# A mixture-of-experts stage cut into 63 tiles of 256 rows and nine of 128, in place of 71 tiles of 256

## The chip, the cores and the metric

The kernel runs on one core of one Trainium2 chip. The metric is the device time of one execution in microseconds. The core has five engines with their own instruction streams: TensorE (PE, matmuls; PEld are its weight loads), VectorE (DVE), ScalarE (ACT), GpSimd (POOL) and SyncE (SP), and 16 DMA engines that all of them feed.

## What is computed

The reference is one layer of a language model over 64 sequences of 128 tokens, with 192 channels:

```python
h = tok(x, adj_cooc, ...)            # embeddings + three graph vectors, projection, layer norm
h = h + attn(layernorm(h))           # a long convolution along each sequence
h = h + ffn(layernorm(h))            # mixture of experts, below

# ffn: E = 8 experts, F = 768 hidden, top 2
router_logits = einsum('th,eh->te', xf, Wr)
topk_vals, topk_idx = top_k(router_logits, 2)
routing_weights = softmax(topk_vals)
h = gelu(einsum('th,efh->etf', xf, Wi) + bi)      # each expert: 192 -> 768 -> 192
expert_out = einsum('etf,ehf->eth', h, Wo) + bo
out = sum over the 2 chosen experts of weight * expert_out
```

8,192 tokens choose two experts each, so 16,384 rows go through the experts. The change is in this last part alone.

## The kernel before

Up to about 460 us the kernel makes h, stores it to `out` in DRAM (`store_rows`), and stores each token's normalised row with its two routing weights in a table `xtab_d`. The experts' weights lie split in a high and a low bf16 part in `blob_d`, 1.44 MB each.

**Placement.** VectorE turns the experts' row counts (bank 0) and each row's rank within its expert (bank 7) into a slot for every row (`sl`, line 1280). An expert's rows begin at a tile's start, so it takes its count, rounded up to 256. `NT` = 71 tiles hold the worst case, and `NC` = 142 blocks of 128 slots. `eid[q]` is the expert of tile q; a tile that no expert needs takes expert 7. A one-hot matmul loop of 16 turns (VectorE line 1297, ScalarE line 956, TensorE line 741) then inverts the slots into a table of row ids, `id_g` to gather with and `id_s` to scatter with. Unused slots scatter to spare rows behind the output.

**Expert stage.** Tile q passes through the engines so, each in its own program order:

- GpSimd: `fetch(q)` gathers two blocks of 128 rows from `xtab_d` (two DMAs, line 537); `add_rows(q)` adds two blocks of results to `out` in DRAM (two accumulating scatters, line 551). In the turn of tile q it issues `fetch(q + 5)` and then `add_rows(q - 2)`. A token's two results are added by different tiles, so a tile's scatters wait until those of the two tiles before it have landed in DRAM. For the last `LATE` = 8 tiles the wait for the tile just before falls away if it has the same expert (`held`).
- ScalarE: `row_hi(q + 1)` (line 963) splits a gathered tile, then `hidden(q)`: twelve gelu activations (lines 975, 976) that end each half bank of the up projection.
- VectorE: `row_lo(q + 1)` (lines 1346, 1347), `split_hidden(q)` (line 1362, three times), `transposed(q + 1)` (line 1351) and `bias_out(q - 1)` (lines 1372, 1376). `bias_out(q)` writes into one of `RY` = 4 output buffers, so it waits until the scatters of tile q - 4 have landed.
- TensorE: `up_tile(q)`, 30 matmuls of 256 columns (lines 780 to 784), `turn_rows(q + 1)`, six transposes (line 763), `down_tile(q - 1)`, 36 matmuls of 192 columns (lines 799 to 801), half of them for each block of 128 rows.
- SyncE: two weight buffers, used by even and by odd tiles. Before tile q it compares `eid[q]` with `eid[q - 2]`, and only if they differ it loads the up part (line 458, 771 KB, once the gelus of tile q - 2 are done) and the down part (line 461, 672 KB, once `bias_out(q - 2)` has read its bias):

```python
sp.wait_ge(gelu, FC // 2 * (q - WB + 1))
with sp.If(e != held):
    load_up(e, w)
```

The inputs are drawn with a fixed seed. Running the reference on them gives the experts 554, 3420, 325, 0, 2312, 718, 2992 and 6063 rows. Before, they take 3, 14, 2, 0, 10, 3, 12 and 24 tiles, 68 in all, and three tiles are empty. `eid[q]` differs from `eid[q - 2]` at twelve tiles: 3, 4, 17 to 20, 29, 30, 32, 33, 44 and 45.

Of the kernel before, what the change touches and what calls it, by code (L numbers as in the profile page):

```python
# [6 lines left out]
B, S, D = 64, 128, 192  # L7
V = 30522
GRAPHS, GD = 3, 16
E, F = 8, 768  # L10
# [11 lines left out]
TS = 256  # L22
NT = (2 * B * S + E * (TS - 1)) // TS
NC = NT * TS // 128
# [12 lines left out]
W3 = 3  # L37
WB = 2
# [3 lines left out]
RX = 6  # L42
# [13 lines left out]
LATE = 8  # L56


def tower(nc, t, out):
# [3 lines left out]
    with ctx:  # L63
# [55 lines left out]
        cst = sb("cst", [128, 128 + 128 + 256 + 128 + 1 + NC + 2 * TG])  # L119
# [13 lines left out]
        onesf = sb("onesf", [128, E])  # L133
# [74 lines left out]
        cnt = carve(4 * E).rearrange("p (a e) -> p a e", a=4)  # L208
# [5 lines left out]
        cnti = sb("cnti", [128, 2, E], i32)  # L214
# [10 lines left out]
        late = sb("late", [1, LATE], i32)  # L225
# [116 lines left out]
        def landed_by(q):  # L342

            return 16 * (q // 2 + 1)
# [6 lines left out]
        def _(sp):  # L351
# [148 lines left out]
            for h in range(2):  # L500
                for a in range(2):
                    sp.wait_ge(scat[h][a], landed_by(NT - 1 - (NT - 1 - a) % 2))

        @block.gpsimd
        def _(pool):
# [28 lines left out]
            def fetch(q):  # L534
                after(pool, hid, q - RX + 1)
                for h in range(2):
                    pool.indirect_dma_start(xg_f[:, q % RX, h, :], None, xtab_d,  # L537
                                            bass.IndirectOffsetOnAxis(ap=id_g[:, 2 * q + h:2 * q + h + 1], axis=0)).then_inc(xg_in[q % RX], 16)

            def add_rows(q):  # L540

                before = held[q] if q in held else landed_by(q - 1)
                for h in range(2):
                    if q > 1:
                        pool.wait_ge(scat[h][q % 2], landed_by(q - 2))
                    if q > 0:
                        pool.wait_ge(scat[h][(q - 1) % 2], before)
                        pool.sem_inc(pool_turn, 1)
                pool.wait_ge(yo_ready, q + 1)
                for h in range(2):  # L550
                    pool.indirect_dma_start(out, bass.IndirectOffsetOnAxis(ap=id_s[:, 2 * q + h:2 * q + h + 1], axis=0), yo[:, q % RY, h, :], None,  # L551
                                            compute_op=ALU.add).then_inc(scat[h][q % 2], 16)
# [7 lines left out]
            held = {NT - LATE + k: pool.value_load(late[0:1, k:k + 1], min_val=landed_by(NT - LATE - 3), max_val=landed_by(NT - 2)) for k in range(LATE)}  # L560
# [12 lines left out]
        def _(pe):  # L573
# [184 lines left out]
            def turn_rows(q):  # L758

                pe.wait_ge(x_lo, q + 1)  # L760
                for h in range(2):
                    for c in range(3):
                        last = nc.tensor.transpose(xT_ps[:, c * TS + h * 128:c * TS + h * 128 + 128],  # L763
                                                   xs[:, q % 2, h, c * 128:(c + 1) * 128], identb[:, :])
                last.then_inc(xg_t, 1)

            def up_tile(q):
# [5 lines left out]
                x0, x1, x2 = (xgT[:, q % W3, c, :] for c in range(3))  # L773
                for f in range(FC):
                    if f % 2 == 0:
                        after(pe, gelu, FC // 2 * (q - 1) + f // 2 + 1)
                    ps = bank[2 + f // 2][:, (f % 2) * TS:(f % 2 + 1) * TS]
# [10 lines left out]
            def down_tile(q):  # L788
# [5 lines left out]
                for h in range(2):  # L794
# [19 lines left out]
        def _(act):  # L814
# [143 lines left out]

            def row_hi(q):

                act.wait_ge(xg_in[q % RX], 32 * (q // RX + 1))
                after(act, xg_t, q - 1)
                f(xs[:, q % 2, :, 0:D], xg_f[:, q % RX, :, 0:D], ACT.Copy).then_inc(x_hi, 1)
# [4 lines left out]
            def hidden(q, w):  # L968

                bi = parts(wbuf[q % WB])[2]  # L970
                for c in range(0, FC, 2):
                    act.wait_ge(up, FC // 2 * q + c // 2 + 1)
                    for d in (c, c + 1):
                        ps = bank[2 + c // 2][:, (d % 2) * TS:(d % 2 + 1) * TS]
                        f(hh[w][:, d, :], ps, ACT.Gelu, bias=bi[:, d:d + 1])  # L975
                        last = f(hf[w][:, d, :], ps, ACT.Gelu, bias=bi[:, d:d + 1])  # L976
                    last.then_inc(gelu, 1)
# [8 lines left out]
        def _(dve):  # L986
# [18 lines left out]
            v.memset(onesf[:, :], 1.0)  # L1005
# [262 lines left out]
            v.tensor_scalar(cnti[:, 0, :], bank[0][:, 0:E], float(TS - 1), None, ALU.add)  # L1268
            fence()
            v.tensor_scalar(cnti[:, 1, :], cnti[:, 0, :], 8, None, ALU.logical_shift_right)  # L1270
            fence()
            v.tensor_copy(cnt[:, 1, :], cnti[:, 1, :])
            fence()
            v.tensor_tensor_scan(cnt[:, 2, :], onesf[:, 0:E], cnt[:, 1, :], 0.0, ALU.mult, ALU.add)
# [24 lines left out]
            for g in range(TG):  # L1299
# [4 lines left out]
                if g == 1:  # L1304
                    dve.wait_ge(eid_turned, 1)
                    v.tensor_scalar(eid[:, :], bank[1][0:1, 0:NT], float(E - 1), None, ALU.min).then_inc(eid_done, 1)

            raw = bank[1][0:1, :]
            assert (NT - LATE) % 2 == 1
# [4 lines left out]
            v.scalar_tensor_tensor(marks[:, 2, :], marks[:, 0, :], E - 0.5, marks[:, 1, :], ALU.is_lt, ALU.mult)  # L1314
            fence()
            v.tensor_tensor(marks[:, 1, :].rearrange("o (k i) -> o k i", i=2), marks[:, 2, :].rearrange("o (k i) -> o k i", i=2),
                            repeat(cst[0:1, 256:256 + LATE // 2], 2, 2), ALU.add)
            fence()
            v.tensor_scalar(late[:, :], marks[:, 1, :], 16.0, float(landed_by(NT - LATE - 3)), ALU.mult, ALU.add)
# [23 lines left out]
            def row_lo(q):  # L1343
                dve.wait_ge(x_hi, q + 1)
                rows, split = xg_f[:, q % RX, :, :], xs[:, q % 2, :, :]
# [3 lines left out]
            def transposed(q, w):  # L1349
                dve.wait_ge(xg_t, q + 1)  # L1350
                v.tensor_copy(xgT[:, w, :, :], bank[0][:, :].bitcast(bf16)[:, 0:3 * TS].rearrange("p (c n) -> p c n", c=3)).then_inc(xgT_ready, 1)  # L1351

            def weights(q, w):

                for h in range(2):
                    v.scalar_tensor_tensor(wk[:, w, h:h + 1], xg_f[:, q % RX, h, D + 1:D + 2], row_k[:, 2 * q + h:2 * q + h + 1],
                                           xg_f[:, q % RX, h, D:D + 1], ALU.mult, ALU.add)

            def split_hidden(q, w, blocks):
                for c in blocks:  # L1360
                    dve.wait_ge(gelu, FC // 2 * q + c // 2 + 1)
                    last = v.tensor_tensor(hl[w][:, c:c + 2, :], hf[w][:, c:c + 2, :], hh[w][:, c:c + 2, :], ALU.subtract)  # L1362
                return last

            def bias_out(q):

                w, x = q % W3, q % RY
                for h in range(2):
                    if q >= RY:
                        dve.wait_ge(scat[h][q % 2], landed_by(q - RY))  # L1370
                dve.wait_ge(down, q + 1)
                v.tensor_tensor(yo[:, x, :, :], bank[5 + w][:, 0:2 * D].rearrange("p (h d) -> p h d", h=2),
                                repeat(parts(wbuf[q % WB])[5], 1, 2), ALU.add).then_inc(biased, 1)
                fence()
                for h in range(2):
# [72 lines left out]
```

## Time and profile before

| | us |
|---|---|
| runs without the profiler, median of 3 (lowest, highest) | 991.08 (987.75, 995.53) |
| span of the profiled execution, first to last instruction | 995.9 |
| first matmul of expert tile 0 | 502.44 |
| last matmul of the expert stage starts | 979.43 |
| last scatter issued | 987.85 |
| TensorE, VectorE, ScalarE, GpSimd busy | 869.3, 656.0, 536.0, 644.7 |

The page gives no separate device time of the profiled execution; its span is 4.8 us above the median of the other runs. A difference worked out within the span is applied to the median.

### The profile page before, as it was taken

To read this page: it belongs to the slowest core of one execution; us is meant where nothing else is said; L and a number is where in the kernel's file an instruction comes from. 1 tells how busy PE (TensorE), PEld (TensorE's weight loads), DVE (VectorE), ACT (ScalarE), POOL (GpSimd) and SP (SyncE) were. 2 spreads that over 40 slices of the span, in tenths; PEclk is the share of its full clock that TensorE was granted. 3 is DMA by queue.
4 is the path that set the end of the run, shared out by engine and by line. 5 is a ranking of instruction groups with operands and counts; after the bars stand their busy time and mean duration, and the time that the engine had idled before them with its cause. 6 is when DMAs were issued, how large, how long until landed. Compare 5 with 4: busy or idle time off the path is not lost.

```text
span 995.9 us, 22850 instructions
## 1 busy us (share of the span) xinstructions
PE 869.3 (87%) x7469; PEld 822.9 (83%) x7469; DVE 656.0 (66%) x2142; ACT 536.0 (54%) x1271; POOL 644.7 (65%) x552
## 2 busy tenths in 40 slices
PE   3959898998898739893889999999999999999993
PEld 2959898998898738892679999999999989898993
DVE  3167857776867565978756776666667656666662
ACT  1222223213312325599667777777777767677761
POOL 6777777777777300100067886777778768788886
PEclk9957556556756669996699999999999999999997
DMA  8437547457465429855946446745744543343454
GB/s 245 131 87 248 179 153 257 136 200 225 157 207 195 126 86 282 225 166 131 245 101 149 61 60 158 191 61 122 199 83 63 130 96 61 59 60 59 61 57 44
DMA packets 99788, 138.31 MB, mean 139 GB/s; under 512 B 13427, under 2 KB 81430, under 8 KB 97654
## 3 DMA queue, kind: packets, MB, share of 16 engines
q0 software_dynamic: 39552, 53.26, 28.1%
q1 hardware_dynamic: 59142, 73.59, 24.3%
q10 hardware_dynamic: 1008, 10.34, 2.8%
q8 instruction: 50, 0.82, 0.4%
q14 instruction: 36, 0.29, 0.1%
HBM read 98.14 MB, written 39.02 MB: 138 GB/s over the span
## 4 chain that ended last, share of the span: by engine, by line
PE 29%; DMA 22%; POOL 22%; issue 12%; DVE 8%; ACT 4%; DVEq 2%; SPq 1%; POOLq 0%; ACTq 0%
DMA out<-Hs,id_s 20%; POOL ev_g L521 13%; POOL emb_g L512 5%; PE bank L799 3%; PE bank L801 3%; PE bank L800 3%; POOL blob L537 3%; PE bank L780 2%; PE bank L781 2%; PE bank L784 2%; PE bank L783 2%; PE bank L782 2%; DVE hstats L1157 2%; ACT adj_s L956 1%; PE bank L763 1%
## 5 line engine op out<-in xcount | busy, mean ns | idle before, releaser
L975 ACT ACTIVATE Hs<-bank,U 128x256 bf16<-128x256 f32 x426 | 214.0, 502 | 126.0 <-PE bank L784 126.0
L551 POOL DMA_INDIRECT out<-Hs,id_s x142 | 233.5, 1645 | 65.6 <-issue 45.6
L537 POOL DMA_INDIRECT blob<-xtab_d,id_g x142 | 151.6, 1068 | 122.7 <-DVEq L1340 79.6
L521 POOL DMA_INDIRECT ev_g<-in_word_emb,ids_i x192 | 189.7, 988 | 58.5 <-issue 57.9
L976 ACT ACTIVATE Hs<-bank,U 128x256 f32<-128x256 f32 x426 | 216.4, 508 | 0.0
L799 PE MATMUL bank<-U,Hs 128*128 128x192 bf16 x852 | 210.0, 246 | 0.3 <-issue 0.3
L801 PE MATMUL bank<-U,Hs 128*128 128x192 bf16 x852 | 208.8, 245 | 0.0
L800 PE MATMUL bank<-U,Hs 128*128 128x192 bf16 x852 | 208.5, 245 | 0.0
L1362 DVE TENSOR_TENSOR Hs<-Hs 128x512 bf16<-128x512 f32 x213 | 146.8, 691 | 92.1 <-ACT Hs L976 92.0
L780 PE MATMUL bank<-wst,U 128*128 128x256 bf16 x426 | 116.6, 274 | 1.3 <-DVE wst L1351 1.3
L781 PE MATMUL bank<-wst,U 128*128 128x256 bf16 x426 | 116.7, 274 | 0.0
L782 PE MATMUL bank<-wst,U 128*128 128x256 bf16 x426 | 116.6, 274 | 0.0
L784 PE MATMUL bank<-wst,U 128*128 128x256 bf16 x426 | 116.6, 274 | 0.0
L783 PE MATMUL bank<-wst,U 128*128 128x256 bf16 x426 | 116.6, 274 | 0.0
L621 PE MATMUL bank<-cs,ev_g 128*128 128x1 f32 x384 | 91.2, 307 | 3.2 <-DMA ev_g<-in_word_emb,ids_i 3.1
L622 PE MATMUL bank<-cs,ev_g 128*128 128x1 f32 x384 | 92.6, 311 | 0.0
L621 PEld LDWEIGHTS bank<-cs,ev_g 128*128 128x128 f32 x384 | 84.0, 270 | 3.4 <-DMA ev_g<-in_word_emb,ids_i 3.4
L622 PEld LDWEIGHTS bank<-cs,ev_g 128*128 128x128 f32 x384 | 85.8, 275 | 0.0
L800 PEld LDWEIGHTS bank<-U,Hs 128*128 128x128 bf16 x852 | 83.5, 98 | 0.0
L799 PEld LDWEIGHTS bank<-U,Hs 128*128 128x128 bf16 x852 | 82.8, 97 | 0.5 <-issue 0.5
L801 PEld LDWEIGHTS bank<-U,Hs 128*128 128x128 bf16 x852 | 82.6, 97 | 0.0
L512 POOL DMA_INDIRECT emb_g<-in_word_emb,ids_i x64 | 64.7, 1011 | 21.8 <-issue 18.3
(216 smaller groups left out, 1643.2 us busy)
## 6 DMA issues: line engine op xcount, KB each, us to landing
adj_s<-in_adj SPq DMA_DIRECT2D x48, 256.0 KB, 7.3
ev_g<-kpad_d SPq DMA_DIRECT2D x24, 512.0 KB, 5.8
U<-blob_d SPq DMA_DIRECT2D x14, 771.0 KB, 5.0
wst<-in_wsrc SPq DMA_DIRECT2D x8, 1344.0 KB
blob_d<-blob ACTq DMA_DIRECT2D x7, 1443.0 KB
U<-blob_d SPq DMA_DIRECT2D x14, 672.0 KB, 5.7
xtab_d<-U SPq DMA_DIRECT2D x4, 1552.0 KB, 17.0
out<-Hs SPq DMA_DIRECT2D x4, 1536.0 KB, 12.8
```

What stands on the lines that cost most here:

```text
L521: pool.indirect_dma_start(ev_g[:, p, j, b, :], None, t["word_emb"], bass.IndirectOffsetOnAxis(ap=ids_i[:, 1 + j, i * Q + b:i * Q + b + 1], ...
L537: pool.indirect_dma_start(xg_f[:, q % RX, h, :], None, xtab_d, bass.IndirectOffsetOnAxis(ap=id_g[:, 2 * q + h:2 * q + h + 1], axis=0)).the ...
L551: pool.indirect_dma_start(out, bass.IndirectOffsetOnAxis(ap=id_s[:, 2 * q + h:2 * q + h + 1], axis=0), yo[:, q % RY, h, :], None, compute_ ...
L621: mm(bank[3][:, k:k + 1], ev_g[:, p, j, b, 0:D0], cs[:, p, k:k + 1], start=True, stop=True)
L622: last = mm(bank[3][:, 16 + k:17 + k], ev_g[:, p, j, b, D - 128:D], cs[:, p, k:k + 1], start=True, stop=True)
L781: mm(ps, hi[:, a], x2, start=False, stop=False)
L799: mm(ps, hh[w][:, f, n], hi[:, c], start=f == 0, stop=False)
L800: mm(ps, hh[w][:, f, n], lo[:, c], start=False, stop=False)
L801: last = mm(ps, hl[w][:, f, n], hi[:, c], start=False, stop=f == FC - 1)
L975: f(hh[w][:, d, :], ps, ACT.Gelu, bias=bi[:, d:d + 1])
L976: last = f(hf[w][:, d, :], ps, ACT.Gelu, bias=bi[:, d:d + 1])
L1362: last = v.tensor_tensor(hl[w][:, c:c + 2, :], hf[w][:, c:c + 2, :], hh[w][:, c:c + 2, :], ALU.subtract)
```

## The change

The block of 128 rows becomes the unit. There are now `NC` = 135 blocks: 63 full tiles of two blocks, and nine single tiles of one, which stand after 3, 10, 18, 26, 34, 41, 48, 55 and 63 full tiles, so that they are tiles 3, 11, 20, 29, 38, 46, 54, 62 and 71 of 72. An expert takes as many pairs of blocks as its rows need where a last odd block is left out, and its odd block, if any, goes to a block behind all the pairs. Pairs fill the full tiles in order; the single tiles are the last nine block numbers. A pair that no longer fits in the full tiles lies in two single tiles. Each stage works on a tile's own width: 30 up matmuls of 128 columns, three transposes, 18 down matmuls, one gather and one scatter in a single tile, and its gelus and differences on half the columns. The counts that a wait asks for follow the tiles' widths (`landed_by(h, q)`), and `held` has a value for each h.

```diff
-NT = (2 * B * S + E * (TS - 1)) // TS
-NC = NT * TS // 128
+NC = (2 * B * S + E * 127) // 128
+SINGLES = E + 1
+FULLS = (NC - SINGLES) // 2
+NT = FULLS + SINGLES
+SINGLE_AFTER = (3, 10, 18, 26, 34, 41, 48, 55, 63)
+def tile_order():
+    order, single = [], 0
+    for full in range(FULLS + 1):
+        for _ in range(SINGLE_AFTER.count(full)):
+            order.append((2 * FULLS + single, 1))
+            single += 1
+        if full < FULLS:
+            order.append((2 * full, 2))
+    return order
+TILES = tile_order()
+def blocks(q):
+    return range(TILES[q][1])
+def width(q):
+    return 128 * TILES[q][1]
+def landed_by(h, q):
+    return 16 * sum(TILES[k][1] > h for k in range(q, -1, -2))
...
             def add_rows(q):
-                before = held[q] if q in held else landed_by(q - 1)
                 for h in range(2):
                     if q > 1:
-                        pool.wait_ge(scat[h][q % 2], landed_by(q - 2))
+                        after(pool, scat[h][q % 2], landed_by(h, q - 2))
                     if q > 0:
-                        pool.wait_ge(scat[h][(q - 1) % 2], before)
+                        after(pool, scat[h][(q - 1) % 2], held[h, q] if (h, q) in held else landed_by(h, q - 1))
                         pool.sem_inc(pool_turn, 1)
                 pool.wait_ge(yo_ready, q + 1)
-                for h in range(2):
+                for h in blocks(q):
...
-                x0, x1, x2 = (xgT[:, q % W3, c, :] for c in range(3))
+                x0, x1, x2 = (xgT[:, q % W3, c, 0:width(q)] for c in range(3))
...
-            v.tensor_scalar(cnti[:, 0, :], bank[0][:, 0:E], float(TS - 1), None, ALU.add)
...
-            v.tensor_tensor(cnt[:, 3, :], cnt[:, 2, :], cnt[:, 1, :], ALU.subtract)
-            v.tensor_scalar(cnt[:, 0, :], cnt[:, 2, :], cst[:, 640:641], None, ALU.is_le)
-            fence()
-            v.tensor_reduce(eidr, cnt[:, 0, :], AX.X, ALU.add).then_inc(experts_at, 1)
-            v.scalar_tensor_tensor(sl, repeat(cnt[:, 3, :], 1, B), float(TS), bank[7][:, :].rearrange("p (b e) -> p b e", e=E), ALU.mult, ALU.add)
+            place = bank[7][:, :].rearrange("p (b e) -> p b e", e=E)
+            v.tensor_scalar(cnti[:, 0, :], bank[0][:, 0:E], 127.0, None, ALU.add)
+            fence()
+            v.tensor_scalar(cnti[:, 1, :], cnti[:, 0, :], 7, None, ALU.logical_shift_right)
+            v.tensor_scalar(cnti[:, 2, :], cnti[:, 0, :], 8, None, ALU.logical_shift_right)
...
+            v.scalar_tensor_tensor(cnt[:, 4, :], pairs_of, -2.0, ends, ALU.mult, ALU.add)
+            v.tensor_scalar(pair_end, total, float(FULLS), total, ALU.max, ALU.add)
...
+            v.tensor_tensor(beyond, place, repeat(edge[:, 0, :], 1, B), ALU.is_ge)
...
+            v.scalar_tensor_tensor(sl, repeat(edge[:, 1, :], 1, B), float(TS), place, ALU.mult, ALU.add)
...
+            v.tensor_tensor(beyond, beyond, repeat(cnt[:, 1, :], 1, B), ALU.mult)
+            v.tensor_reduce(eidr, reached.rearrange("p a e -> p (a e)"), AX.X, ALU.add).then_inc(experts_at, 1)
+            fence()
+            v.scalar_tensor_tensor(sl, beyond, float(TS), sl, ALU.mult, ALU.add)
```

GpSimd, expert stage, before: the issues around any tile (out is written by the scatters, blob holds the gathered rows; in brackets the semaphores waited for).

```order
L551 DMA out<-Hs,id_s 8704x192 [waits scat01,scat00,scat11,scat10,yo_ready]
L551 DMA out<-Hs,id_s 8704x192
L537 DMA blob<-xtab_d,id_g 128x194 [waits hid]
L537 DMA blob<-xtab_d,id_g 128x194
L551 DMA out<-Hs,id_s 8704x192 [waits scat00,scat01,scat10,scat11,yo_ready]
```

The same place now, around the scatter of single tile 38:

```order
L581 DMA blob<-xtab_d,id_g 128x194 [waits hid]
L581 DMA blob<-xtab_d,id_g 128x194
L595 DMA out<-Hs,id_s 8704x192 [waits scat00,scat01,scat10,scat11,yo_ready]
L581 DMA blob<-xtab_d,id_g 128x194 [waits hid]
L595 DMA out<-Hs,id_s 8704x192 [waits scat01,scat00,scat11,scat10,yo_ready]
L595 DMA out<-Hs,id_s 8704x192
```

One scatter and one gather (that of single tile 46) stand between two waits for landed scatters, where two and two stood. The number of such waits per tile is the same.

VectorE, placement, before: from the counts to the slots (cnti and ev_g hold small counts and the slots, bank the counts and ranks).

```order
L1268 TENSOR_SCALAR cnti<-bank 128x8 [waits ranks]
L1270 TENSOR_SCALAR cnti<-cnti 128x8
L1272 CAST ev_g<-cnti 128x8
L1274 SCALAR_TENSOR_TENSOR ev_g<-onesf,ev_g 128x8
L1276 TENSOR_TENSOR ev_g<-ev_g 128x8
L1277 TENSOR_SCALAR ev_g<-ev_g,cst 128x8
L1279 TENSOR_REDUCE ev_g<-ev_g 128x1
L1280 SCALAR_TENSOR_TENSOR ev_g<-ev_g,bank 128x512
```

Now, the second half of it:

```order
L1339 TENSOR_TENSOR ev_g<-bank,ev_g 128x512
L1341 SCALAR_TENSOR_TENSOR ev_g<-ev_g 128x8
L1342 SCALAR_TENSOR_TENSOR ev_g<-ev_g,bank 128x512
L1344 SCALAR_TENSOR_TENSOR ev_g<-ev_g 128x8
L1345 TENSOR_SCALAR ev_g<-ev_g,cst 128x8
L1347 TENSOR_TENSOR ev_g<-ev_g 128x512
L1348 TENSOR_REDUCE ev_g<-ev_g 128x1
L1350 SCALAR_TENSOR_TENSOR ev_g<-ev_g 128x512
```

Eight instructions became twenty, of which twelve stand ahead of the part shown, all of 16 columns or fewer; four instead of one are 512 columns wide.

## Rows read from the trace of the kernel before

**Rows 1.** The page's fourth part: the chain that ended last, by line.
```profile
DMA out<-Hs,id_s 20%; POOL ev_g L521 13%; POOL emb_g L512 5%; PE bank L799 3%; PE bank L801 3%; PE bank L800 3%; POOL blob L537 3%; PE bank L780 2%; PE bank L781 2%; PE bank L784 2%; PE bank L783 2%; PE bank L782 2%; DVE hstats L1157 2%; ACT adj_s L956 1%; PE bank L763 1%
```

**Rows 2.** Timeline, TensorE, one period: start, duration, engine, line, output and input.
```profile
699.68 0.27 PE L780 MATMUL bank<-wst,U 128*128 128x256 bf16 x1
...
702.95 0.50 PE L763 MATMUL bank<-identb,wst 128*128 128x128 bf16 x6
...
706.26 0.27 PE L780 MATMUL bank<-wst,U 128*128 128x256 bf16 x1
```

**Rows 3.** TensorE: two later starts of an up projection; its waits from 500 us.
```profile
798.52 0.27 PE L780 MATMUL bank<-wst,U 128*128 128x256 bf16 x1
...
956.68 0.27 PE L780 MATMUL bank<-wst,U 128*128 128x256 bf16 x1
...
PE bank L763 <- DVE wst L1347: 8.1, 5, 4.1
```

**Rows 4.** Timeline, GpSimd, one calm period.
```profile
757.38 1.63 POOL L551 DMA_INDIRECT out<-Hs,id_s  x1 [0.30 <-issue]
759.31 1.59 POOL L551 DMA_INDIRECT out<-Hs,id_s  x1 [0.30 <-issue]
761.20 1.18 POOL L537 DMA_INDIRECT blob<-xtab_d,id_g  x1 [0.30 <-issue]
762.68 0.98 POOL L537 DMA_INDIRECT blob<-xtab_d,id_g  x1 [0.30 <-issue]
763.97 1.63 POOL L551 DMA_INDIRECT out<-Hs,id_s  x1 [0.30 <-issue]
```

**Rows 5.** Line 551, issue to landing: windows 540 to 600, then 783 to 809.
```profile
DMA to landing us min/median/max: 3.5/3.6/4.2
...
DMA to landing us min/median/max: 4.9/6.1/7.7
```

**Rows 6.** Timeline, SyncE's queue: first and last of four weight loads.
```profile
784.93 0.34 SPq L458 DMA_DIRECT2D U<-blob_d  x1
...
800.87 0.34 SPq L461 DMA_DIRECT2D U<-blob_d  x1
```

**Rows 7.** GpSimd: first scatters of tiles 0, 13, 17, 24, 31, 38, 42, 63; the last scatter.
```profile
516.85 2.01 POOL L551 DMA_INDIRECT out<-Hs,id_s  x1 [3.68 <-DVE Hs L1376]
...
605.83 1.63 POOL L551 DMA_INDIRECT out<-Hs,id_s  x1 [0.30 <-issue]
...
637.08 1.91 POOL L551 DMA_INDIRECT out<-Hs,id_s  x1 [1.15 <-DMA out<-Hs,id_s]
...
683.36 1.76 POOL L551 DMA_INDIRECT out<-Hs,id_s  x1 [0.30 <-issue]
...
737.50 1.73 POOL L551 DMA_INDIRECT out<-Hs,id_s  x1 [0.30 <-issue]
...
783.74 1.63 POOL L551 DMA_INDIRECT out<-Hs,id_s  x1 [0.30 <-issue]
...
816.16 1.63 POOL L551 DMA_INDIRECT out<-Hs,id_s  x1 [0.30 <-issue]
...
958.62 1.63 POOL L551 DMA_INDIRECT out<-Hs,id_s  x1 [0.30 <-issue]
...
987.85 1.55 POOL L551 DMA_INDIRECT out<-Hs,id_s  x1 [0.30 <-issue]
```

**Rows 8.** VectorE, the end of a tile's row_lo.
```profile
701.56 0.42 DVE L1347 TENSOR_TENSOR wst<-blob,wst 128x256 bf16<-128x256 f32 x1
```

**Rows 9.** VectorE, the placement: its first row, its last two.
```profile
460.02 0.16 DVE L1268 TENSOR_SCALAR cnti<-bank 128x8 int32<-128x8 f32 x1
...
461.45 0.68 DVE L1280 SCALAR_TENSOR_TENSOR ev_g<-ev_g,bank 128x512 f32<-128x512 f32 x1
462.20 1.23 DVE L1282 TENSOR_TENSOR ev_g<-ev_g 128x1024 f32<-128x1024 f32 x1
```

**Rows 10.** TensorE, forty 128-column matmuls in a row, at full clock.
```profile
494.80 2.41 PE L750 MATMUL bank<-identb,zero_f 128*128 128x128 bf16 x40 [0.75 <-DVEq L1340]
```

More of the change, by code:

```diff
@@ L56, with block_of @@
 LATE = 8
+def tile_order():
[10 more added lines that the diff above has]
+    return range(TILES[q][1])
+def block_of(q, h):
+    return TILES[q][0] + h
+def width(q):
+    return 128 * TILES[q][1]
+def landed_by(h, q):
+    return 16 * sum(TILES[k][1] > h for k in range(q, -1, -2))
+assert len(TILES) == NT and 2 * FULLS + SINGLES == NC
+assert all(TILES[q][1] == 2 for q in range(NT - LATE - 1, NT - 1))
 def tower(nc, t, out):
@@ L224, in tower @@
         marks = sb("marks", [1, 3, LATE])
-        late = sb("late", [1, LATE], i32)
+        late = sb("late", [1, 2, LATE], i32)
+        expert_row = sb("expert_row", [1, 2, NT])
         tp = old_adj[:, 0:2 * CC * 128].rearrange("p (a c t) -> p a c t", a=2, c=CC)
@@ L559, in _ @@
                 fetch(q)
-            held = {NT - LATE + k: pool.value_load(late[0:1, k:k + 1], min_val=landed_by(NT - LATE - 3), max_val=landed_by(NT - 2)) for k in range(LATE)}
+            held = {(h, NT - LATE + k): pool.value_load(late[0:1, h, k:k + 1], min_val=landed_by(h, NT - LATE + k - 3), max_val=landed_by(h, NT - LATE + k - 1))
+                    for h in range(2) for k in range(LATE)}
             pool.wait_ge(h_out, 16 * (NG + 1))
@@ L760, in turn_rows @@
                 pe.wait_ge(x_lo, q + 1)
-                for h in range(2):
+                for h in blocks(q):
                     for c in range(3):
@@ L793, in down_tile @@
                 after(pe, biased, q - W3 + 1)
-                for h in range(2):
+                for h in blocks(q):
                     ps = bank[5 + w][:, h * D:(h + 1) * D]
@@ L957, in _, with fetched_by @@
                 last.then_inc(hot_s_ready, 1)
+            def fetched_by(q):
+                return 16 * sum(TILES[k][1] for k in range(q, -1, -RX))
             def row_hi(q):
-                act.wait_ge(xg_in[q % RX], 32 * (q // RX + 1))
+                act.wait_ge(xg_in[q % RX], fetched_by(q))
                 after(act, xg_t, q - 1)
-                f(xs[:, q % 2, :, 0:D], xg_f[:, q % RX, :, 0:D], ACT.Copy).then_inc(x_hi, 1)
+                f(xs[:, q % 2, 0:TILES[q][1], 0:D], xg_f[:, q % RX, 0:TILES[q][1], 0:D], ACT.Copy).then_inc(x_hi, 1)
             row_hi(0)
@@ L1344, in row_lo @@
                 dve.wait_ge(x_hi, q + 1)
[L1345 removed]
+                rows, split = xg_f[:, q % RX, 0:TILES[q][1], :], xs[:, q % 2, 0:TILES[q][1], :]
                 v.tensor_tensor(split[:, :, D:D + D1], rows[:, :, D0:D], split[:, :, D0:D], ALU.subtract)
@@ L1409 @@
     cst = np.concatenate([np.eye(128, dtype=np.float32), (r[:, None] < r[None, :]).astype(np.float32),
-                          np.tile(np.arange(256, dtype=np.float32), (128, 1)), np.tile(t[::-1], (128, 1)), r[:, None],
+                          np.tile(np.arange(256, dtype=np.float32), (128, 1)), np.tile(t[::-1], (128, 1)),
+                          np.array([first for first, _ in TILES] + [float(NC)] * (128 - NT), np.float32)[:, None],
                           (B * S + r[:, None] + 128 * (np.arange(NC) % (SPARE // 128))[None, :]).astype(np.float32),
                           np.ldexp(np.float32(128) + r[:, None], np.concatenate([np.arange(TG) + B * k for k in range(2)])[None, :])
-                          .astype(np.float32)], axis=1)
+                          .astype(np.float32),
+                          np.tile(np.array([landed_by(h, NT - LATE + k - 3) for h in range(2) for k in range(LATE)], np.float32), (128, 1))], axis=1)
     Wi, Wo = a["L0_ffn_Wi"], a["L0_ffn_Wo"]
```

92 lines of the change are left out of this document (57 added, 35 removed).

## The prediction

> **What bounds the kernel now.** I read the page's chain of waits first, because every engine looks busy. Its largest item is no matmul but the accumulating scatter into the output, a fifth of the whole span [rows 1]. Then I read the expert stage, where the change is, engine by engine.
>
> TensorE first. A tile's up projection starts at 699.68, its transposes at 702.95 and the next up projection at 706.26 [rows 2]: 6.58 us for a tile, 3.27 of it the 30 matmuls of 256 columns, without a gap. The starts at 798.52 and 956.68 [rows 3] are 23 tiles apart: 158.16 / 23 = 6.88 us. At 6.59 (6.58 and 6.60 take turns) they would be 151.6 apart, so TensorE loses 6.6 us there. It waits for VectorE's row_lo [rows 3], and that stands behind bias_out, which waits for landed scatters. GpSimd is what holds it up.
>
> GpSimd then. In a calm stretch it issues a scatter, 1.93 us later the second, then two gathers, and the next tile's scatter 6.59 us after the first [rows 4]. Between issues it sits idle for 0.30 us only: it is as full as TensorE. The first gather took 1.18 us, the second 0.98. With 0.98 for both the four issues would need 1.93 + 1.89 + 1.28 + 1.29, or 6.39 us; so it can hardly catch up anything.
>
> What puts it behind? From 605.83 to 637.08 it does four tiles, from 683.36 to 737.50 seven, and from 783.74 to 816.16 four [rows 7]: 4.9, 8.0 and 6.1 us more than 6.59 each. These are the stretches in which experts change and SyncE loads weights; four such loads lie between 784.93 and 800.87 [rows 6]. A scatter lands 3.6 us after its issue in a calm stretch and 6.1 us (up to 7.7) beside the loads [rows 5], and the next tile's scatter waits for it. Where GpSimd issues two scatters and two gathers, that wait is hidden up to about 4.2 us; above that each microsecond is lost. Four output buffers let it fall about three tiles behind before VectorE and TensorE stall, which happens from about 800 us on. From 816.16 to 958.62 it does 21 tiles in 142.5 us, 6.78 each [rows 7], and then TensorE goes at GpSimd's pace. Its last scatter is issued 8.4 us after the last matmul starts. So the end of the kernel is the sum of what GpSimd does between its first scatter at 516.85 and its last at 987.85, and I make the sum there.
>
> **The change part by part, on GpSimd's path.**
>
> Fewer blocks. Seven scatters of 142 go, each 1.93 us to the next issue [rows 4]: 13.5 us. Seven gathers go; that of single tile 3 lies before the first scatter, beside other waits, so six count, at 1.29 us (0.98 and the 0.30 to the next issue): 7.7 us. Together -21.2.
>
> Placement. The VectorE steps from the counts to the slots take 462.20 - 460.02 = 2.2 us before [rows 9]. One of them is 128x512, 0.75 us to the next start. Now there are four, hence +2.25. The small ones grow from seven to sixteen. The seven took 461.45 - 460.02 = 1.4 us, 0.2 each with the drains between them; the nine new ones mostly share a drain with another, so I count 0.1 each, +0.9. The one-hot loop behind works on 5% fewer blocks, an estimated -0.6. No other work covers the chain: the row ids are the last thing that the first gather waits for. I take +2.5, bounds 1.5 to 4. It shifts everything behind it.
>
> Waits for landing around single tiles. The new order puts one gather between two scatter groups once for each of eight single tiles that are gathered during the loop: either the scatter of a single tile stands just before it (tile 38, then the gather of 46), or a full tile's second scatter does. The next scatter is then ready 1.93 + 1.30 = 3.23 us after the last one, but that lands after 3.6 [rows 5], and the wait and the 0.30 between issues follow: about 0.65 us lost. Eight times that is +5, bounds 0 (if landing is hidden by the time the issue itself needs) and 8 (where a load stands beside it).
>
> Weight loads. This is the term with the largest weight. I place the experts' counts by the new rule. They need 2, 13, 1, 0, 9, 3, 12 and 24 pairs, 64 in all, but there are 63 full tiles. So the last pair of expert 7 falls into single tiles 3 and 11, both in the middle of expert 1. The odd blocks of experts 0, 1, 2 and 4 fall into tiles 20, 29, 38 and 46, in the middle of experts 4, 5, 6 and 7. Only tiles 54, 62 and 71 are empty and take expert 7, as their neighbours do. Each of the six strangers makes SyncE load its expert into one of the two buffers and the old expert again two tiles later. `eid[q]` differs from `eid[q - 2]` at tiles 2, 3, 5, 11, 13, 17 to 20, 22, 28, 29, 31, 32, 33, 38, 40, 45, 46 and 48: twenty tiles in place of twelve, 16 transfers more of some 0.7 MB. The rows of before give the price: 4.9 + 8.0 + 6.1 us in the three stretches, for ten of the twelve. The other two fall between tiles 0 and 13, which take 89.0 us [rows 7], 3.3 more than 13 x 6.59; 2.6 of these are one tile's two gathers more than scatters, as the lead grows, and 0.7 remain. That is 19.7 us for twelve, 1.6 each, and +13 for eight more. A count by time: loads are in flight over about 33 tiles instead of 19, at 19.7 / 19 = 1.04 us, +14. I take +14, because the twenty fall on all phases of the loop. Bounds: the price of the two at the start, 0.35 each (+3), and of the third stretch, 3.0 each (+24).
>
> Pace while behind. GpSimd took 6.78 us for a tile when the others waited for it, and 6.59 before that. With more loads early it is behind from about tile 25 instead of 41. That is at most 16 tiles at 0.19 more, +3; some of it is in the price of the loads already. I take +1, bounds 0 and 5.
>
> The Trainium skill names a mechanism for this (SBUF — State Buffer, "Who interferes with whom"): certain VectorE instructions hold a port pair that GpSimd needs to write descriptors, and GpSimd blocks for their whole duration. The gather of 1.18 us beside one of 0.98 [rows 4] agrees. By the Trainium skill the 0.2 us would come once for every tile wherever the phases lock, so this term would be +3 rather than +1, and the sum +3.3.
>
> TensorE. Seven blocks less are 7 x 3.29 = 23 us less work. None of it shows while GpSimd sets the end. In a single tile it will also wait: row_lo ends at 701.98, 2.30 us after the up projection's start [rows 2, 8], while a half-wide up projection takes 1.65 us (half of 3.27, or 30 matmuls at the 56 ns at which forty of 128 columns follow each other [rows 10]); 0.65 us for each of nine single tiles, 6 us of the 23 lost. Weights may come late too: a load of the up part is issued after the gelus of tile q - 2, and a stranger's down load and the next up load overlap, 1.44 MB; up to 1 us for each of six. Both are covered by GpSimd's lag, and cost 12 us if that cover is gone.
>
> ScalarE and VectorE lose work in single tiles and are bound nowhere; GpSimd's sixteen register loads for `held` in place of eight stand beside the first gathers: 0.
>
> **Sum.** -21.2 + 2.5 + 5 + 14 + 1 = +1.3 us on 995.9. On the median of 991.08 that is 992.4; I say 992. A measurement of this kernel tells about 1% (10 us) from no change; this is no change.
>
> **Rivals.**
>
> *The scatter chain gets shorter, faster.* If a load costs half of the mean (0.8 us, +6) and half the landing waits are hidden, the sum is -21.2 + 2.5 + 2.5 + 6 = -10, 981. For it: early in the stage GpSimd is not yet behind, and some load time falls where it waits for TensorE anyway; the loads are spread, and one transfer alone disturbs one scatter. Against it: the third stretch, with only two tiles that load, cost most. The floor is TensorE's own pace: 979.7 - 6.6 - 23 + 2.5 + 6 to 12 is 958.6 to 964.6 for its end, and 9.4 us behind that for the last block and the tail (1.4 to its scatter, as for the tile before, 8.05 from there to the span's end), so 968 to 974 on the span, 963 to 969 on the median. To get there GpSimd would have to lose less in twenty loads than it did in twelve.
>
> *The strangers' loads cost what the third stretch cost, slower.* Eight more at 3.0 us are +24: the sum is +11, 1002. The mechanism: the stranger's down load and the reload of the up part follow each other within 3 us, scatters beside two overlapping transfers land after 7 us rather than 5, and with a single tile's one scatter and one gather less cover stands in front of the wait. From 2.8 us each it is over 1%. If the landing waits at the single tiles also come to 8, 1005.
>
> **How the numbers follow.** No change within 1%, by the sum: 0.46, with its own range 983 to 1001. Faster, by the first rival: 0.27, of which the floor has 0.05. Slower, by the second: 0.27. The sum of all lower bounds is -21.2 + 1.5 + 0 + 3 + 0 = -17 (974), of all upper ones -21.2 + 4 + 8 + 24 + 5 = +20 (1011). They will hardly all meet; the range is 976 to 1008. Faster by over 1% is under 981.2, slower is over 1001.
>
> **What the profile after would show.** GpSimd's last scatter is again the last link of the chain of waits, at about 989 us of a span of 997. The first scatter is near 519.5. SyncE has twenty loads of each part in the expert stage, not twelve. The scatters around tiles 3, 11, 20, 29, 38 and 46 land after 5 to 7 us. VectorE's bias_out waits for landed scatters from about tile 25 on, for more than the 44 us in all of before. TensorE's half-wide up matmuls stand 55 ns apart. I am wrong if TensorE runs without waits to the end (the first rival), or if scatters beside a single load are as quick as calm ones, or if the waits between scatters at single tiles are far from 0.65 us.

## The result, and the profile after

The changed kernel takes 1002.23 us (median of 4 runs, 999.02 to 1003.29) beside 991.86 for the kernel before. The ratio is 1.0091, interval 1.0059 to 1.0124: about 9 us slower. The slowdown is clear of noise, but the interval does not settle whether it is under 1%. The point forecast was 992, the range 976 to 1008.

The profiled execution of the changed kernel has a span of 1001.5 us. The one of before, from which the rows ahead of the prediction come, happened to be long: a second profile of the same kernel has a span of 988.1. Therefore differences are told below by ratios of timed runs, with 992 us as the unit, and spans serve to find the place.

First the path on which the sum was made. From the page of the changed kernel, and then of the second profile of before, the scatters and the gathers (count, busy time, mean ns, idle time ahead of them in us):

```profile
L595 POOL DMA_INDIRECT out<-Hs,id_s x135 | 225.5, 1670 | 88.6 <-issue 64.2
L581 POOL DMA_INDIRECT blob<-xtab_d,id_g x135 | 138.3, 1025 | 128.1 <-DVEq L1410 82.7
```

```profile
L551 POOL DMA_INDIRECT out<-Hs,id_s x142 | 234.8, 1653 | 62.4 <-issue 42.8
L537 POOL DMA_INDIRECT blob<-xtab_d,id_g x142 | 149.2, 1051 | 121.4 <-DVEq L1340 78.3
```

GpSimd works 9.3 us less on scatters and 10.9 less on gathers, but it waits 26.2 us longer ahead of its scatters. What was saved is there, and more than that went into waiting.

Who waits for whom in the expert stage of the changed kernel (total us, times, longest):

```profile
DVE Hs L1444 <- DMA out<-Hs,id_s: 74.6, 33, 6.5
POOL out L595 <- issue: 64.2, 107, 3.8
...
PE bank L808 <- DVE wst L1417: 26.9, 20, 3.5
```

Line 1444 is bias_out: it waits 74.6 us for landed scatters, where line 1372 waited 44.0 in the first profile of before and 37.4 in the second. TensorE waits 26.9 us for the row_lo that stands behind it, against 8.1 [rows 3] and 2.8 in the second profile. TensorE waits for no weight load anywhere in the expert stage.

GpSimd's timeline, its first and its last scatter, which answer to [rows 7]:

```profile
519.53 1.81 POOL L595 DMA_INDIRECT out<-Hs,id_s  x1 [0.69 <-DVE Hs L1448]
...
994.38 1.55 POOL L595 DMA_INDIRECT out<-Hs,id_s  x1 [0.31 <-issue]
```

Now one stranger. Single tile 11 takes expert 7 amid expert 1's tiles. First its four weight loads on SyncE's queue (up and down of tile 11, up and down of tile 13), then GpSimd from the scatters of tile 8 on, then the landing of the scatters issued between 575 and 580 us (the trace has it for the second of the two alone):

```profile
567.89 0.34 SPq L501 DMA_DIRECT2D U<-blob_d  x1
576.10 0.34 SPq L504 DMA_DIRECT2D U<-blob_d  x1
579.10 0.34 SPq L501 DMA_DIRECT2D U<-blob_d  x1
588.24 0.34 SPq L504 DMA_DIRECT2D U<-blob_d  x1
```

```profile
576.41 1.63 POOL L595 DMA_INDIRECT out<-Hs,id_s  x1 [0.30 <-DVE Hs L1448]
578.34 1.59 POOL L595 DMA_INDIRECT out<-Hs,id_s  x1 [0.30 <-issue]
580.23 1.02 POOL L581 DMA_INDIRECT blob<-xtab_d,id_g  x1 [0.30 <-issue]
581.56 1.01 POOL L581 DMA_INDIRECT blob<-xtab_d,id_g  x1 [0.30 <-issue]
586.42 2.08 POOL L595 DMA_INDIRECT out<-Hs,id_s  x1 [3.84 <-issue]
...
DMA to landing us min/median/max: 7.3/7.3/7.3
```

The loads at 576.10 and 579.10 start 3 us apart. The scatter issued between them at 578.34 takes 7.3 us to land rather than 3.6 [rows 5], the next tile's scatter begins 0.8 us after that landing, and from the first scatter of tile 8 to that of tile 9 it is 10.01 us rather than 6.59 [rows 4].

And the gap at a narrow tile where no load is near, tile 46 (its only scatter, the gather of tile 54, the first scatter of tile 47):

```profile
853.45 1.62 POOL L595 DMA_INDIRECT out<-Hs,id_s  x1 [0.30 <-DVE Hs L1448]
855.37 0.99 POOL L581 DMA_INDIRECT blob<-xtab_d,id_g  x1 [0.30 <-issue]
858.04 1.59 POOL L595 DMA_INDIRECT out<-Hs,id_s  x1 [1.68 <-issue]
```

From scatter to scatter it is 4.59 us. The issues alone would take 3.2; I had reckoned 3.9. The landing of this scatter is not in the trace.

### The profile page after: what moved, and what is told of

Read it like the earlier page. It is cut to its first block and busy times, and to the rows that moved or that the text cites. A ratio compares the mean times of both kernels' runs of the same rounds, so it can differ in the third digit from the quotient of the medians.

```text
span 1001.5 us, 22727 instructions
## 1 busy us (share of the span) xinstructions
PE 853.1 (85%) x7352; PEld 805.2 (80%) x7352; DVE 643.3 (64%) x2149; ACT 526.7 (53%) x1284; POOL 623.6 (62%) x538
## 5 line engine op out<-in xcount | busy, mean ns | idle before, releaser
L1024 ACT ACTIVATE Hs<-bank,U 128x256 bf16<-128x256 f32 (+1 forms) x432 | 211.0, 489 | 141.0 <-PE bank L829 141.0
L595 POOL DMA_INDIRECT out<-Hs,id_s x135 | 225.5, 1670 | 88.6 <-issue 64.2
L581 POOL DMA_INDIRECT blob<-xtab_d,id_g x135 | 138.3, 1025 | 128.1 <-DVEq L1410 82.7
L1025 ACT ACTIVATE Hs<-bank,U 128x256 f32<-128x256 f32 (+1 forms) x432 | 213.5, 494 | 0.0
L844 PE MATMUL bank<-U,Hs 128*128 128x192 bf16 x810 | 201.0, 248 | 0.0
L846 PE MATMUL bank<-U,Hs 128*128 128x192 bf16 x810 | 199.9, 247 | 0.0
L845 PE MATMUL bank<-U,Hs 128*128 128x192 bf16 x810 | 199.7, 247 | 0.0
L1434 DVE TENSOR_TENSOR Hs<-Hs 128x512 bf16<-128x512 f32 (+1 forms) x216 | 140.8, 657 | 78.9 <-ACT Hs L1025 78.0
L825 PE MATMUL bank<-wst,U 128*128 128x256 bf16 (+1 forms) x432 | 115.7, 268 | 3.0 <-DVE wst L1421 3.0
L826 PE MATMUL bank<-wst,U 128*128 128x256 bf16 (+1 forms) x432 | 115.6, 268 | 0.0
L828 PE MATMUL bank<-wst,U 128*128 128x256 bf16 (+1 forms) x432 | 115.6, 268 | 0.0
L827 PE MATMUL bank<-wst,U 128*128 128x256 bf16 (+1 forms) x432 | 115.6, 268 | 0.0
L829 PE MATMUL bank<-wst,U 128*128 128x256 bf16 (+1 forms) x432 | 115.5, 267 | 0.0
L1444 DVE TENSOR_TENSOR Hs<-bank,U 128x384 f32<-128x384 f32 (+1 forms) x72 | 38.3, 532 | 89.9 <-DMA out<-Hs,id_s 74.6
L845 PEld LDWEIGHTS bank<-U,Hs 128*128 128x128 bf16 x810 | 80.0, 99 | 0.1
L844 PEld LDWEIGHTS bank<-U,Hs 128*128 128x128 bf16 x810 | 79.3, 98 | 0.1
L846 PEld LDWEIGHTS bank<-U,Hs 128*128 128x128 bf16 x810 | 79.1, 98 | 0.1
```

The source lines that it names most:

```text
L825: mm(ps, hi[:, a], x0, start=True, stop=False)
L844: mm(ps, hh[w][:, f, n], hi[:, c], start=f == 0, stop=False)
L845: mm(ps, hh[w][:, f, n], lo[:, c], start=False, stop=False)
L846: last = mm(ps, hl[w][:, f, n], hi[:, c], start=False, stop=f == FC - 1)
L1024: f(hh[w][:, d, 0:width(q)], ps, ACT.Gelu, bias=bi[:, d:d + 1])
L1025: last = f(hf[w][:, d, 0:width(q)], ps, ACT.Gelu, bias=bi[:, d:d + 1])
```

## The experiments

All ratios are to the kernel before on the same chip. "Strangers" are the six single tiles whose expert differs from that of the tiles around them.

### 1. The same narrow tiles, at home

```diff
-SINGLE_AFTER = (3, 10, 18, 26, 34, 41, 48, 55, 63)
+SINGLE_AFTER = (2, 15, 16, 25, 44, 48, 52, 55, 63)
+SINGLE_BLOCK = (2, 3, 4, 5, 0, 1, 6, 7, 8)
...
-            order.append((2 * FULLS + single, 1))
+            order.append((2 * FULLS + SINGLE_BLOCK[single], 1))
```

> The changed kernel with the single tiles in another order: the odd block of each expert stands beside that expert's full tiles, the two single tiles that take expert 7's last pair stand among expert 7's. Then the expert of tile q differs from that of tile q - 2 at twelve tiles, as before the change, not at twenty; the number of blocks, tiles and instructions stays. Theory A (the strangers' weight loads slow the scatters): 8 x 1.7 = 14 us less than the changed kernel, a span of about 987, 0.5% below the kernel before. Rival B (the narrow tiles themselves cost, by waits for landing and by stalls that follow them): no more than 2 us less, a span of about 1000.

Ratio 0.9953, interval 0.9925 to 0.9981; span 988.5. The order of the tiles alone is worth 1.0091 - 0.9953, or 13.7 us. As far as the order goes, theory A's 14 us hold and B falls. With the strangers at home the change makes the kernel faster, by 0.5%. (The order is written for these inputs' counts.)

### 2. Loads added to the kernel before

Tiles carry a tag beside their expert, and SyncE compares tags.

```diff
+AGAIN = (11, 24, 38, 52)
...
-                e, held = expert(q), expert(q - WB)
+                e, now, held = expert(q), tagged(q), tagged(q - WB)
...
-                with sp.If(e != held):
+                with sp.If(now != held):
```

> The kernel before with four tiles (11, 24, 38, 52) marked so that their expert's weights are loaded again for them and once more two tiles later: twenty tiles that load in place of twelve, all tiles 256 wide, the result the same. Theory A: 14 us more (1.7 for each of the eight), a span near 1010, ratio 1.014; with the price of the third stretch, 3.0 each, 24 us. Rival B: no change, within 3 us, since the loads are hidden and only narrow tiles cost.

Ratio 1.0033, interval 1.0005 to 1.0061: 3.3 us (0.5 to 6) for eight loading tiles, 0.4 each and not 1.7. Taken alone this contradicts theory A as I had stated it: a load has no fixed price. Rival B's "within 3 us" is not ruled out by this run.

### 3 and 4. No loads at all

In both kernels the two `sp.If` branches are replaced:

```diff
-                with sp.If(e != held):
-                    load_up(e, w)
-                with sp.Else():
-                    sp.sem_inc(wi_in[w], 16)
+                sp.sem_inc(wi_in[w], 16)
```

> The changed kernel without any weight load after the first two tiles' (all tiles then use the experts' weights that lie in the two buffers, so most results are of the wrong expert). Compared with the kernel before treated the same way. Theory A: the 20 us of loads and more are gone, and what is left of the change is 21.2 us fewer blocks against 2.7 of placement and 5 of landing waits: a span near 963, 12 to 18 us below the other. Rival B: less than 5 us below the other.

> The kernel before without any weight load after the first two tiles' (most results are of the wrong expert). Theory A: GpSimd keeps its calm pace of 6.59 us for a tile and TensorE loses nothing: a span of 974 to 977. Rival B says the same of this one; if it stays above 985, the stretches in which GpSimd falls behind are not due to the loads.

The changed kernel comes to 0.9828 (0.9791 to 0.9866), the kernel before to 0.9919 (0.9890 to 0.9947). Loads cost the kernel before 8 us and the changed one 26. Without them the change gains 9 us. I had expected 12 to 18, and spans near 963 and of 974 to 977; they are 973.1 and 981.8. The narrow tiles cost more than the 5 us in my sum, and without loads the kernel before keeps TensorE's pace, 6.59 us for a tile, from the first scatter to the last, so it can gain no more than its 8 us.

### 5. Loads at the strangers' places, in full tiles

> The kernel before, all tiles 256 wide, with tiles 3, 11, 20, 29, 38 and 46 marked to load their expert's weights again, and once more two tiles later: the places at which the changed kernel has its six strangers, next to the same expert boundaries. 21 tiles load in place of twelve. Theory C (it is the crowding of loads at expert boundaries that makes a stranger dear): about 14 us more than the kernel before. Theory N (it is that the stranger's tile is narrow): 3 to 4 us more, as for marks at four places apart (ratio 1.0033).

The edit is `AGAIN = (3, 11, 20, 29, 38, 46)`. Ratio 1.0046 (1.0015 to 1.0077), 4.6 us for nine more loading tiles, 0.5 each. The places alone are not what makes strangers dear; theory C falls.

### 6 and 7. Marks on narrow and on full tiles, far from boundaries

Tags as in 2, in the kernel of experiment 1, with `AGAIN = (48, 53, 58, 62)` (narrow) and `(50, 55, 59, 64)` (full).

> The kernel with the single tiles beside their experts' tiles, and its four narrow tiles 48, 53, 58 and 62 marked to load their own expert's weights again and once more two tiles later: twenty loading tiles, far from expert boundaries. Theory N: 8 x 1.7 = 14 us above that kernel (ratio to the kernel before about 1.009). Theory C: 3 us above it (ratio 0.998).

> The same with four full tiles 50, 55, 59 and 64 marked, in the same stretch. Theory N: 3 us above the kernel without marks (ratio 0.998), 11 us below the one with the narrow tiles marked. Theory C: the same as that one. Theory L (a load costs what it costs only where GpSimd is already several tiles behind, whatever the width): both about equal and 8 us or more above the kernel without marks.

Ratios 1.0015 (0.9983 to 1.0047) and 0.9994 (0.9957 to 1.0031), that is 6.2 and 4.1 us above the kernel without marks. The intervals overlap, so the 2 us between them are not settled, and each difference is uncertain by about 4 us. Neither comes near 14. Theory N is at most a part: late in the stage a narrow tile's load costs about 0.8 us, not 1.7. Theory L, which had 8 us or more for both, is not borne out by the medians; the intervals do not exclude it.

### 8. The kernel before, profiled again

> The kernel before, unchanged, for a second profile: its first profiled execution had a span of 995.9, near the slowest of its runs, while the other kernels' spans lie 1 to 3 us below their median. If that was chance, this span is 988 to 993 and GpSimd waits less than 22 us ahead of its scatters.

The span is 988.1, as expected if the first profile was long by chance. The waits ahead of the scatters are 62.4 us instead of 65.6 (19.8 instead of 23 beyond the 0.30 ahead of each), so only a small part of the 7.8 us; the first scatter is 4.5 us earlier.

### 9. The changed order without the strangers' loads

```diff
+SHIFT = {3: -6.0, 11: -6.0, 20: 4.0, 29: 4.0, 38: 4.0, 46: 3.0}
...
+                    v.tensor_tensor(expert_row[:, 1, :], expert_row[:, 1, :], shift, ALU.add)
```

> The changed kernel in its own order, but the six strangers' tiles (3, 11, 20, 29, 38, 46) are given the expert of the tiles around them, so that eleven tiles load and not twenty (the 7 or so in a hundred of the rows that lie in these tiles get the wrong expert). It keeps the spacing of the narrow tiles, which the kernel with the narrow tiles at home changed together with the loads. Theory A (the loads of the strangers are all of the 14 us between the two orders): the same as the order at home, ratio 0.995. Rival S (narrow tiles every eight or nine tiles, so that a narrow gather meets a narrow scatter, cost a part): ratio 1.000 to 1.005.

(By the experts' counts the six tiles hold 386 of the 16,384 rows, 2.4 in a hundred and not seven.) Ratio 0.9924, interval 0.9898 to 0.9950. In the same order of narrow and full tiles, the strangers' nine loading tiles cost 1.0091 - 0.9924, or 16.6 us, 1.8 each. The spacing of the narrow tiles costs nothing that shows beside the order at home (0.9924 against 0.9953, the intervals overlap); rival S falls.

### 10 to 12. Waiting for the previous tile's scatters only where the expert changes

```diff
-LATE = 8
+LATE = 64
...
+            def held(h, q):
+                k = q - NT + LATE
+                if k < 0:
+                    return landed_by(h, q - 1)
+                return pool.value_load(late[0:1, h, k:k + 1], min_val=landed_by(h, q - 3), max_val=landed_by(h, q - 1))
...
-                        after(pool, scat[h][(q - 1) % 2], held[h, q] if (h, q) in held else landed_by(h, q - 1))
+                        after(pool, scat[h][(q - 1) % 2], held(h, q))
```

The table `late` is filled for 64 tiles, with the step of a wait by the width of the tile before. The kernel before has `LATE = 63` and one value for both blocks.

> The kernel with the narrow tiles at home, in which tiles 8 to 71 and not the last eight alone wait for the scatters of the tile just before them only if the expert changes there (one expert's tiles share no token). GpSimd loads two registers more for each tile. Theory W (what costs is the wait for the previous tile's scatters to land, which loads and narrow tiles make longer): the waits ahead of the scatters fall from 33 us to under 10, TensorE sets the pace, ratio 0.970 to 0.980. Rival R (GpSimd is full by its own instructions, and 0.1 to 0.2 us more for each tile's registers take back what the waits gave): ratio 0.990 to 1.000.

> The changed kernel in its own order with the same relief. A stranger still makes two waits, at itself and at the tile behind it. Theory W: ratio 0.975 to 0.985, so that 4 to 6 of the 14 us between the two orders remain. Rival R: ratio above 1.000.

> The kernel before, with the same relief for tiles 8 to 70. Theory W: as without any loads, ratio 0.990 to 0.993, bound by TensorE at 6.59 us a tile; then the change is worth 12 to 20 us once the waits are gone. Rival R: ratio 1.000 or above.

At home 0.9820 (0.9782 to 0.9858), the changed order 0.9849 (0.9811 to 0.9887), the kernel before 0.9927 (0.9899 to 0.9954). Rival R falls. At home the ratio stays just above the 0.970 to 0.980 of theory W. The kernel before is as fast as without any load (0.9919): as far as these runs can tell, the loads cost it time only through this wait. The two orders are now 3 us apart instead of 14, less than the 4 to 6 expected, and their intervals overlap. In its own order the change is now worth 0.9927 - 0.9849, or 8 us, and at home 11; I had expected 12 to 20. The kernel at home is the fastest that computes the right result, 974.5 us in median, 18 us under the kernel before.

Its waits, and those of the kernel before with the same relief:

```profile
DVE Hs L1452 <- DMA out<-Hs,id_s: 4.8, 15, 0.3
```

```profile
DVE Hs L1375 <- DMA out<-Hs,id_s: 11.3, 35, 0.3
```

bias_out no longer waits for landed scatters in either, beyond a step of 0.3 us, so GpSimd no longer holds up TensorE. In the changed order with the relief it still waits 31.4 us for them, against 74.6. The waits ahead of the scatters fall at home from 73.7 to 66.0 us, that is from 33 to 25.5 beyond the 0.30 ahead of each, and not to under 10 as I wrote; the largest part of what is left is now GpSimd's waiting for results:

```profile
POOL out L603 <- DVE Hs L1456: 16.2, 13, 3.7
```

### Where in the stage the time goes

From GpSimd's timelines I took each scatter's start, less the first one's, less 3.295 us (half of TensorE's 6.59) for each scatter before it. The table gives that lag in us after so many scatters:

```
scatters   before  before again  exp. 5  changed  exp. 1  exp. 9  exp. 10
      12      3.4           3.4     3.4      6.1     5.5     3.8      6.2
      24      3.5           3.4     6.4     15.2     6.2     6.8      3.3
      30      7.2           7.4     8.0     22.4    12.6     9.6      3.5
      54     13.9          14.0    19.2     33.8    29.5    19.5     16.4
      72     16.5          14.9    21.3     40.7    30.2    24.1     16.8
      96     24.0          23.3    27.1     49.9    34.3    30.0     13.4
     120     26.4          23.9    26.9     52.9    40.3    32.9     17.0
```

The changed kernel is 20.0 us behind experiment 9 after 120 scatters. Of these, 8.4 us are lost by scatter 24, which begins at 613.81 us and so before the third stranger's first load (625.21): that is the harm of the strangers in tiles 3 and 11. Marks on full tiles at the same places (experiment 5) cost 3.0 us by scatter 24. Another 4.4 are lost by scatter 30, while the loads of tiles 20 and 22 start. Experiment 5's lag of 5 to 6 us in the middle shrinks to 3.0 at the end beside the second profile of before. My reading, not shown by itself, is that the kernel before loses there in its own way what the other has lost earlier.

The same timelines give the whole account between the first and the last scatter: the issues with the 0.30 behind each, and the idle time beyond, split into the gaps between two tiles' scatters that have a single gather in them, and the rest (us, each row from one profile).

```
              total  issues  idle: at single gathers  elsewhere
before again  467.7   449.0                      0.0       18.7
exp. 9        454.8   425.8                      8.0       21.0
changed       474.9   426.5                      9.3       39.0
```

The change saves 22.5 us of issues. It adds 9.3 us of idle time at single gathers and 20.3 elsewhere, and 18.0 of these are not there in experiment 9, which lacks the strangers' loads alone.

## Why the prediction was right, point by point

The step that decides, that GpSimd's chain of scatters sets the end and not TensorE's work, was right, and so was the reason named for the loss: the strangers' loads delay landings for which the next scatter waits. Every term can now be set beside a measurement. The two largest costs, at single tiles and for loads, came out higher than I had put them, and the load term has its size by luck.

**Fewer blocks, -21.2.** In the table above the issues, with the 0.30 behind each, fall by 22.5 us between the first and the last scatter, in seven scatters and six gathers. Right, to about 1 us.

**Placement, +2.5.** On VectorE, the first row and the one behind the last step, which answer to [rows 9]:

```profile
459.52 0.16 DVE L1320 TENSOR_SCALAR cnti<-bank 128x8 int32<-128x8 f32 x1
...
465.11 1.23 DVE L1352 TENSOR_TENSOR ev_g<-ev_g 128x1024 f32<-128x1024 f32 x1
```

5.6 us, 3.4 more than before. The first scatter, which I had written "near 519.5", is 2.7 us later than in [rows 7], but 7.2 later than in the second profile of before, since the stage does not begin at the same time in every execution. Counted from the first placement step it comes after 55.8 to 56.8 us in the six profiles of kernels with full tiles only, and after 59.2 to 61.0 in six of kernels with single tiles, on average 3.7 us later. So the term is +3.7, inside its bounds, and the 0.6 us that I had set off for the shorter one-hot loop do not show.

**Waits at single tiles, +5.** Mis-sized: 8.0 us in experiment 9, 9.3 in the changed kernel. In experiment 9 the seven gaps with one gather lose 0.8 to 1.3 us each, 1.15 on average, where I had put 0.65. At the eighth, behind tile 63, nothing is lost (0.01), because for the last eight tiles the wait for the tile just before falls away. The step that was off is the last one: to the landing of 3.6 us I had added the 0.30 between issues, but in ten waits of the changed kernel whose landing the trace has, the waiting scatter begins 0.8 to 0.95 us after it. 3.6 + 0.8 to 0.95 less 3.2 is 1.2 to 1.35. The ratio of experiment 9 leaves room for 10 us: -7.5 with nearly as many loads as before, against -21.2 + 3.7.

**Loads, +14.** 13.7 us by experiment 1 and 16.6 by experiment 9. The size was right, but by luck. The reason behind it, a price of 1.7 us for any loading tile, was wrong: full tiles pay 0.4 to 0.5 (experiments 2 and 5), and the mean of before hid that some loads pay 3 and some nothing. That the strangers' loads cost near that mean did not follow from it.

**Pace while behind, +1.** The gathers' mean did not rise but fell, from 1051 to 1025 ns on the pages above. So the stretched gather in every tile while GpSimd is behind, which I had drawn from the Trainium skill (SBUF — State Buffer, "Who interferes with whom"), did not show. The rows do not bear out its mechanism as I cited it either. The VectorE instructions beside the gather of 1.18 us [rows 4] are tensor_tensors of lines 1347 and 1362, and the Trainium skill, in the same section, gives tensor_tensor no mode that takes the whole port pair, only contention with GpSimd's reads if both inputs are in SBUF. In the first profile of before, gathers that overlap line 1362 took 1.12 us on average, the others 1.00; in the changed kernel, 1.06 and 1.00 beside line 1434. That is a stretch of about 0.1 us beside an instruction of 0.69 us with both inputs in SBUF, not a block for its whole duration. The pace in all, in the table of lags, is still 0.2 to 0.25 us a tile above TensorE's between scatters 96 and 120, in the changed kernel (3.0 us in 12 tiles) as in the first profile of before (2.4), though hardly so in the second (0.6). What more tiles at it cost was not measured apart from the other waits.

The account does not need my terms. Issues -22.5, placement +3.7, single gathers +9.3, idle elsewhere +20.3, and 0.9 less behind the last scatter (7.1 against 8.05 us) make +9.9, beside 9 by the ratio and +1.3 in my sum. The forecast of no change within 1% was right by a hair, which is luck too: the point was 8 us too low by the ratio and 10 by the median, and the ratio's interval reaches past 1%. The rival that was nearest is the slower one. Its condition, 2.8 us for each stranger's load, did not hold: by experiments 1 and 9 it is 1.7 to 1.8.

**TensorE, covered.** The half-wide up projection runs as worked out, 29 steps in 1.62 us, 56 ns each:

```profile
632.06 0.22 PE L825 MATMUL bank<-wst,U 128*128 128x128 bf16 x1
...
633.68 0.22 PE L829 MATMUL bank<-wst,U 128*128 128x128 bf16 x1
...
634.29 0.51 PE L808 MATMUL bank<-identb,wst 128*128 128x128 bf16 x6 [0.39 <-DVE wst L1417]
```

The wait for row_lo behind it is 0.4 to 0.6 us where GpSimd is not in the way, against 0.65 predicted. The late weights for which I had set aside up to 6 us never made TensorE wait.

**The signs I had named.** Twenty loads of each part, a last scatter 7 us ahead of the span's end, and waits of bias_out above 44 us and from tile 19 on (I wrote 25) are there. The last scatter was predicted at 989 and is at 994.38. Landings of 5.0 to 7.3 us are there too, but not where I had put them: of the 31 landings that the trace has, the six long ones belong to scatters of tiles 8, 10, 14, 24, 36 and 40. Next to tiles 3, 20, 29 and 46 they are 3.5 to 4.6. SyncE starts a stranger's loads before GpSimd comes to its scatter, those of tile 11 for instance while GpSimd is at tiles 6 to 8.

**What stays open.** A stranger's load costs 1.8 us, a mark on a full tile 0.5 at the same places, a mark on a narrow tile late in the stage about 0.8. Why is open. Narrowness and an early place go together in tiles 3 and 11, where 8 of the 20 us are lost, and at tile 11 two loads fell on a pair of scatters. A kernel with marks on narrow home tiles at those places would tell whether it is the width or that coincidence; it was not run.

## What to carry to other kernels

Ask what orders the work that looks like background: here the wait for an accumulating scatter to land, not the matmuls, turned 5% fewer blocks into 1% more time. A split of work into finer tiles is paid in the neighbourhood of each odd tile, in weights exchanged twice and in fixed latencies with less work to hide them, so price the neighbours and not only the tile. And when a wait guards against a conflict that most neighbours cannot have, remove it first: with it gone the same change was worth 8 us (0.9927 against 0.9849) instead of costing 9, and 11 with the narrow tiles at home (0.9820).

## What the runs showed of the hardware

- A weight load of 0.7 MB had no fixed price on the scatters. A scatter issued while two loads started 3 us apart landed after 7.3 us instead of 3.6, one issued 0.7 us behind a single load (754.68 us) after 4.7. The twelve loads of before cost 8 us in one kernel and, with the wait relieved, nothing measurable.
- From the landing of one scatter to the start of the one that waits for it 0.8 to 0.95 us passed (ten waits of the changed kernel), nearly three times the 0.30 us between issues that wait for nothing.
- Gathers that overlapped a VectorE tensor_tensor of 0.69 us with both inputs in SBUF took about 0.1 us longer on average (1.12 against 1.00 us in the first profile of before).
- Loading a wait's value from memory into a register, once for each tile on GpSimd, cost too little to be seen where TensorE sets the pace: the kernel before with it is as fast as the kernel before without weight loads (0.9927 and 0.9919). Where GpSimd sets the pace it was not tried by itself.
